# Feed-forward lists of a four-layer decoder: eight buffers of fetched rows with a lead of six, the best two experts by maxima, a BF16 inversion of places, and the weights in the last products

## What is computed

```python
# layer 0: h = rms-normed x
logits = h @ gate_w.T
top_w, top_i = top_k(softmax(logits), 2);  top_w /= top_w.sum(-1)
out[t] = sum over its two experts e of top_w * (silu(h @ w1[e].T) * (h @ w3[e].T)) @ w2[e].T
# layer 2
logits = x @ gate_w + gate_b
gw, top_i = softmax(top_k(logits, 2)), top_k(logits, 2)
out[t] = sum over its two experts e of gw * (gelu(x @ w1[e] + b1[e]) @ w2[e] + b2[e])
out[t] += gelu(x @ ws1 + bs1) @ ws2 + bs2
```

## Time and profile before

| | us |
|---|---|
| median of 3 runs | 3127.24 |
| the profiled execution | 3124.51 |
| its span | 3122.7 |
| PE busy | 2618.2 (84%) |
| DVE, ACT, POOL busy | 1691.0, 1106.2, 951.8 |
| layer 0: its feed-forward stage `Lists`, start to the end of the last product | 567 to 904 |
| layer 2: the same | 1946 to 2276 |

### The profile page before, as it was taken

The page is one execution under the profiler, slowest core; times in us unless marked ns, Lnnn a source line. Parts: engine busy times, 40 slices in busy tenths (PEclk is TensorE's granted clock), DMA queues, the critical chain, the costliest instruction groups (busy, mean ns, idle before and its releaser), DMA issues. The chain is left out here.

```text
span 3122.7 us, 39578 instructions
## 1 busy us (share of the span) xinstructions
PE 2618.2 (84%) x15186; PEld 1487.0 (48%) x15186; DVE 1691.0 (54%) x2983; ACT 1106.2 (35%) x2411; POOL 951.8 (30%) x953
## 2 busy tenths in 40 slices
PE   7999997656669998878888888866589999997999
PEld 3545555544444443446565655444443333333556
DVE  4454426411127871467777774412147878896623
ACT  1333333111115672233455553311134343433422
POOL 3332302032221100142544551122204444442265
PEclk8999989687878999989899998855669999999999
DMA  2000001100020002165222222100000000001033
GB/s 93 1 1 1 1 20 56 31 17 19 19 74 1 1 1 86 45 148 146 75 62 55 59 74 102 64 20 19 22 25 1 1 1 1 1 1 46 1 123 108
DMA packets 48353, 126.47 MB, mean 41 GB/s; under 512 B 11251, under 2 KB 26486, under 8 KB 44438
## 3 DMA queue, kind: packets, MB, share of 16 engines
q1 hardware_dynamic: 41638, 110.56, 11.2%
q0 software_dynamic: 6528, 13.38, 1.6%
HBM read 97.67 MB, written 26.23 MB: 40 GB/s over the span
## 5 line engine op out<-in xcount | busy, mean ns | idle before, releaser
L327 ACT ACTIVATE work<-ps 128x512 f32<-128x512 f32 (+5 forms) x959 | 496.2, 543 | 1130.3 <-PE ps L317 678.9
L317 PE MATMUL ps<-parts 64*128 64x512 f32 (+9 forms) x4368 | 829.7, 425 | 66.7 <-ACT fw_sb L328 15.0
L317 PEld LDWEIGHTS ps<-parts 32*128 32x128 f32 (+3 forms) x4368 | 450.5, 191 | 455.8 <-issue 227.3
L347 DVE TENSOR_REDUCE fw_sb<-ps 128x2 f32<-128x1024 f32 (+3 forms) x384 | 414.6, 1085 | 269.2 <-PE ps L317 268.7
L317 PE MATMUL ps<-fw_sb,work 128*32 128x128 f32 (+4 forms) x2174 | 397.7, 401 | 6.6 <-ACT work L327 2.2
L317 PE MATMUL ps<-work 128*32 128x256 f32 (+7 forms) x2524 | 380.2, 415 | 19.6 <-DVE work L331 11.1
L321 PE MATMUL ps<-wc_sb,work 128*128 128x128 f32 (+3 forms) x910 | 184.5, 328 | 236.8 <-DMA work<-scr_rows,work 189.6
L327 ACT ACTIVATE fw_sb<-ps 128x512 f32<-128x512 f32 (+5 forms) x394 | 204.6, 537 | 289.5 <-PE ps L317 246.9
L321 PEld LDWEIGHTS ps<-wc_sb,work 128*128 128x128 f32 (+3 forms) x910 | 129.0, 166 | 348.9 <-DMA work<-scr_rows,work 270.3
L344 DVE COPY work<-ps 128x512 f32<-128x512 f32 (+3 forms) x139 | 91.2, 660 | 342.8 <-PE ps L321 293.5
L317 PEld LDWEIGHTS ps<-fw_sb,work 128*32 128x32 f32 (+2 forms) x2174 | 219.2, 182 | 86.4 <-issue 72.4
(11 more groups left out here) (147 smaller groups left out, 3268.8 us busy)
## 6 DMA issues: line engine op xcount, KB each, us to landing
work<-scr_places SPq DMA_DIRECT2D x64, 256.0 KB
work<-scr_w SPq DMA_DIRECT2D x15, 1024.0 KB, 4.6
work<-scr_sk SPq DMA_DIRECT2D x64, 128.0 KB, 2.7
scr_sp<-wr_sb SPq DMA_DIRECT2D x64, 128.0 KB, 2.2
fw_sb<-in_f SPq DMA_DIRECT2D x1, 6528.0 KB, 19.3
fw_sb<-in_f SPq DMA_DIRECT2D x1, 5632.0 KB, 16.2
fw_sb<-in_f SPq DMA_DIRECT2D x1, 4608.0 KB, 18.3
scr_rows<-work SPq DMA_DIRECT2D x4, 1024.0 KB, 6.8
```

Of the source, the lines that this page charges most:

```text
L317: return self.e.matmul(o, l, r, start=start, stop=stop) if self.e else Unwritten()
L327: return self.e.activation(o, i, f, bias=bias, scale=scale)
L347: return self.e.tensor_reduce(o, i, AX.X, op, negate=neg) if self.e else Unwritten()
```

## The change

- `Lists` has eight buffers of fetched rows for four, six gathers ahead of the loop for three, and gathers n+6 for n+3; a buffer is free once `turn_pe` has read list n-8.
- The class `ListRoute` is gone. `choose_dve` finds the best expert by a maximum, takes it out, and finds the second the same way; where two are equal, the constant `order` picks the earlier one. ACT takes the exponential of 128x16 numbers in place of 128x128, behind all four copies of the tokens.
- `hot`, `of` and `V` are BF16, with the tokens innermost. `V` holds the token's number in two parts, which DVE adds afterwards, and no weights. Three BF16 constants are made once, by POOL in the first norm of the program.
- Weights: `weights_dve` runs behind the places. ACT makes 32 diagonal tiles from them, one in each turn of the loop from n = 2, and `back_pe` multiplies by these in place of the identity. `output_act` no longer scales.
- In layer 2 `prefix_pe` is set at 1, `inverted_pe` at 6 to 9 and `row_pe` at 11 to 14.

```diff
-        self.fetched = [k.event(f"fetched{l}_{i}", 16) for i in range(4)]
+        self.fetched = [k.event(f"fetched{l}_{i}", 16) for i in range(8)]
...
-        self.rows, self.X, self.S, self.out = ring(4, 128), ring(3, 128), ring(2, 512), ring(4, 128)
+        self.rows, self.X, self.S, self.out = ring(8, 128), ring(3, 128), ring(2, 512), ring(4, 128)
...
     def inverted_pe(self, e, q):
+        e.wait_ge(*k.made_v[t, "totals"])
         e.wait_ge(*k.made_v[t, "hot", q])
-        for i in range(8 * q, 8 * q + 8):
-            ins = e.matmul(r.Mb[1][:, 0:n], self.hot[:, tile(i)], self.V[:, n * i:n * i + n], start=i == 0, stop=i == 31)
+        for i in range(8):
+            n = 8 * q + i
+            ins = e.matmul(self.Mb[1][:, 0:2 * N], view(self.hot[:, 1024 * q + i:], [8, 128]), view(self.V[:, n:], [32, 2 * N]),
+                           start=n == 0, stop=n == 31)
...
     def shared_pe(self, e):
-            if i == 3:
+            if i == 1:
                 self.prefix_pe(e)
-            if 7 <= i < 11:
-                self.row_pe(e, i - 7)
-            if 10 <= i < 14:
-                self.inverted_pe(e, i - 10)
+            if 6 <= i < 10:
+                self.inverted_pe(e, i - 6)
+            if 11 <= i < 15:
+                self.row_pe(e, i - 11)
...
     def back_pe(self, e, c):
-                ins = e.matmul(k.ps[c][:, tile(i)], self.yt[:, at:at + 128], k.cst("id"), start=self.l == 0 and j == 0,
+                ins = e.matmul(k.ps[c][:, tile(i)], self.yt[:, at:at + 128], self.diag[:, tile(16 * j + 4 * c + i)], start=self.l == 0 and j == 0,
...
     def output_act(self, e, n):
-        e.activation(self.out[n % 4], self.Y, ACT.Copy, scale=self.w[:, n:n + 1]).then_inc(*k.made_a.up((t, "output", n)))
+        e.activation(self.out[n % 4], self.Y, ACT.Copy).then_inc(*k.made_a.up((t, "output", n)))
+
+    def diagonal_act(self, e, m):
+        e.wait_ge(*k.made_v[t, "weights"])
+        e.wait_ge(*k.summed[t, "inverted", 3])
+        e.activation(self.diag[:, tile(m)], k.cst("id"), ACT.Copy, scale=self.wk[:, m:m + 1]).then_inc(*k.made_a.up((t, "diagonal", m)))
...
+    def choose_dve(self, e):
+        e.wait_ge(*k.summed[t, "logits"])
+        self.step(e, e.reduce(self.m1, by_e(L), ALU.max))
+        self.step(e, e.tt(by_e(d), by_e(L), each(self.m1), ALU.subtract), (t, "logits"))
+        self.step(e, e.stt(by_e(tie), by_e(d), 0.0, order, ALU.is_equal, ALU.mult))
+        self.step(e, e.reduce(self.c16, by_e(tie), ALU.max))
+        self.step(e, e.tt(by_e(one), by_e(tie), each(self.c16), ALU.is_equal))
+        self.step(e, e.stt(d, one, -BIG, d, ALU.mult, ALU.add))
+        self.step(e, e.reduce(self.m2, by_e(d), ALU.max))
+        self.step(e, e.tt(by_e(d2), by_e(d), each(self.m2), ALU.subtract), (t, "second"))
+        self.step(e, e.stt(by_e(tie), by_e(d2), 0.0, order, ALU.is_equal, ALU.mult))
+        self.step(e, e.reduce(self.c16, by_e(tie), ALU.max))
+        self.step(e, e.tt(by_e(two), by_e(tie), each(self.c16), ALU.is_equal))
+        self.step(e, e.tt(self.mask, one, two, ALU.add), (t, "mask"))
...
     def places_dve(self, e):
+        self.step(e, e.tt(of, each(self.j), view(k.firstb[:, :], [32, N], [1, 32]), ALU.is_equal))
+        e.tt(V(0), of, each(k.pairb[:, 0:32]), ALU.mult).then_inc(*k.made_v.up((t, "lower numbers")))
+        e.tt(V(1), of, each(k.pairb[:, 32:64]), ALU.mult).then_inc(*k.made_v.up((t, "upper numbers")))
...
     def pool(self, e):
-        for n in range(3):
+        for n in range(6):
             self.fetch_pool(e, n)
         e.wait_ge(*k.made_v[t, "to"])
         for n in range(N):
-            if n + 3 < N:
-                self.fetch_pool(e, n + 3)
+            if n + 6 < N:
+                self.fetch_pool(e, n + 6)
             self.send_pool(e, n)
...
@@ class FirstNorm(PickNorm): pool
+        for o, name, n, m in ((k.seqb, "seq", 128, 8), (k.firstb, "firsts", 39, 32), (k.pairb, "pairs", 64, 1)):
+            e.copy(view(o[:, :], [m, n], [1, m]), view(k.cst(name), [1, n], [0, m])).then_inc(*k.made_g.up((self.tag, o.name)))
```

More of the change, by code:

```diff
@@ L3364, in __getitem__, with __init__ @@
         return self.of[name][name]
[L3367 to L3386, removed]
 class Lists(Stage):
     N = 39
-    def __init__(self, k, l, A, route, x, big):
+    def __init__(self, k, l, A, x, big):
         super().__init__(f"lists{l}")
-        self.k, self.l, self.r, self.x = k, l, route, x
+        self.k, self.l, self.x, self.Mb, self.steps = k, l, x, [k.ps[6], k.ps[7]], 0
         self.width = 448 if l == 0 else 512
@@ L3448, in logits_pe @@
     def logits_pe(self, e):
[L3449 to L3452, removed]
+        k, bank, plain = self.k, self.Mb[1], self.l == 0
+        if not plain:
+            e.matmul(bank[:, 0:128], k.cst("ones")[0:1, :], view(k.wt(2, "gateb"), [0, 16], [1, 8]), stop=False)
         for i in range(16):
[L3454 to L3456 removed]
+            ins = e.matmul(bank[:, 8 * i:8 * i + 8], self.x[:, tile(i)], k.wt(self.l, "gate"), start=plain, stop=plain or i == 15)
+        ins.then_inc(*k.summed.up((self.tag, "logits")))
     def tokens_pe(self, e, c):
@@ L3566, in back_pe @@
         e.wait_ge(*self.came[c])
+        e.wait_ge(*k.made_a[t, "diagonal", 31])
         for i in range(4):
@@ L3669, in act @@
                 self.output_act(e, n - 2)
+            if 2 <= n < 34:
+                self.diagonal_act(e, n - 2)
     def step(self, e, ins, key=None):
-        self.r.step(e, ins, key)
+        k = self.k
+        self.steps += 1
+        key = key or (self.tag, "chain", self.steps)
+        ins.then_inc(*k.made_v.up(key))
+        e.wait_ge(*k.made_v[key])
+    def choose_dve(self, e):
+        k, t, L = self.k, self.tag, self.Mb[1]
+        by_e, each = lambda a: view(a, [8, 16], [1, 8]), lambda a: view(a, [1, 16], [0, 8])
+        order = view(k.cst("order"), [0, 16], [1, 8])
+        d, d2, tie, one, two = self.d, self.d2, self.tie, self.sel[:, 0:128], self.sel[:, 128:256]
+        e.wait_ge(*k.summed[t, "logits"])
[11 more added lines that the diff above has]
+        self.step(e, e.tt(self.mask, one, two, ALU.add), (t, "mask"))
@@ L3774, in fetch_pool @@
         k, t = self.k, self.tag
-        e.wait_ge(*k.summed[t, "turned", n - 4])
-        e.gather(self.rows[n % 4], self.table, self.at[:, n:n + 1]).then_inc(*self.fetched[n % 4].up(n))
+        e.wait_ge(*k.summed[t, "turned", n - 8])
+        e.gather(self.rows[n % 8], self.table, self.at[:, n:n + 1]).then_inc(*self.fetched[n % 8].up(n))
     def send_pool(self, e, n):
```

144 lines of the change are left out of this document (70 added, 74 removed).

## The result

| | before | after |
|---|---|---|
| median | 3127.56 us (4 runs, 3119.09 to 3132.26) | 2791.03 us (4 runs, 2779.13 to 2802.17) |
| profiled execution, its span | 3124.51, 3122.7 | 2788.2, 2786.4 |
| granted clock over the span | 0.886 | 0.931 |
| layer 0, loop | 273.6 | 122 |
| layer 2, loop | 261.0 | 105 |

The ratio is 0.8926 with a 95% interval of 0.8884 to 0.8969. The forecast was 2796 us.

What follows compares the result with a forecast made beforehand. The prediction took a ring of output, scatter, gather and PE's turn, with PE's lowered clock, to bound both loops. Terms −19.5 − 149.6 − 158 − 6.2 + 2.6 = −330.7 us gave 2796 us, range 2778 to 2890.

Steps and rivals of the forecast that it cites:

- The loops: Loops over 39 lists: six lists of lead bring layer 0 from 273.6 to 124 us, layer 2 from 261.0 to 103.
- Layer 2's turn: Layer 2's loop: PE's turn 2.3 us at full clock, GpSimd slower, so the loop ends at 101.5 us or later.
- Layer 0 before the loop: Layer 0's start: new mask search, DVE wide operations of 9.1 us and cheaper BF16 inversion save 19.5 us.
- Layer 2 before the loop: Layer 2's inversion in PE's stream: four quarters of 1.91 us become 0.35 us each, 6.2 us less.
- The first norm: End of the first norm's stage: three more POOL casts behind the 2048 cast cost 2.6 us, at worst 5.
- Diagonals: Products behind the loops: diagonals replace the identity in 64 instructions of the same shape, costing 0.
- The stages behind: Stages behind the loops: their end should not move in length.
- (a): Rival, layer 2's loop: PE stays at half clock, 4.6 us a turn, loop 181 us, total 2874 us; chance 0.11.
- (b): Rival, both layers' loops: PE stays at half clock, layer 0's loop 233 us, total 2983 us; chance 0.04.
- (c): Rival, both loops: scatter and gather transfers serialise, 4.9 us a turn, 191 us each, total 2951 us; chance 0.05.
- (d): Rival, both loops: more indirect transfers in flight each take longer, kernel gets slower, 3307 us; chance 0.02.
- (e): Rival, both loops: the lead does nothing, only the starts and the cast count, 3104 us; chance 0.02.

Runs made afterwards that it cites:

- lead_only: Kernel before with only eight buffers of fetched rows and a gather lead of six; 2820.4 us, ratio 0.904.
- lead3: Kernel after with four buffers and a gather lead of three, all other edits kept; 3091.9 us, ratio 0.9911.
- pool1: Kernel after with one memset of 128x512 and a wait for it behind each scatter on GpSimd; 2815.6 us, ratio 0.9017.
- hot_rows: Kernel after with the BF16 one-hot array of places laid out by token tile, its columns side by side; 2797.1 us, ratio 0.8958.
- v_rows: Kernel after with the 78 columns of V for one token tile side by side; 2783.0 us in one run.
- no_diagonal: Kernel after without the 32 diagonals on ACT, identity used again, weights left out of the result; 2802.1 us, ratio 0.8974.
- after_again: Kernel after run once more, unchanged, beside the kernel with three small edits; 2820.2 us, ratio 0.9009.
- pool2: Kernel after with two memsets of 128x512, each waited for, behind each scatter on GpSimd; 2858.2 us, ratio 0.9154.
- lead4: Kernel after with five buffers and a gather lead of four; 2822.3 us, ratio 0.9045.

## Why the prediction was right, and where not

- **The loops** (−149.6 and −158) are the change, and both terms stand: −151.2 and −156.1 us by the traces. lead_only and lead3 show from both sides that the lead is the cause. The turn in layer 0, 3.0 us with 2.93 as the bound, is 2.94.
- **Layer 2's turn** was mis-sized, and the 103 us came out near 104.9 by luck. The prediction had 2.3 us for PE's turn, and it is 2.46. The step at fault is the 1.44 us from a transposition to the next product up: in the loop it is 1.60 (1860.49 to 1862.09), and 0.86 from there to the next transposition, which is the 1.02 less the overlap, as forecast. The 1.44 was read in the earlier trace rows from the turn just before the first scatter; the kernel after also has it in that one turn and 1.60 from the next on. What adds the 0.16 us is not shown. The forecast then took GpSimd's 101.5 us for the bound, over 96 us for PE alone. But PE's own stream fills the 104.9 us: 8.0 us for the first three turns, some 2.47 for each of 36, and 7.9 behind them, where the prediction had 5. GpSimd would have been done some 4 us earlier, as its waits at the loop's end and pool1 show.
- **Layer 0 before the loop** (−19.5) came to −20.45 us, 41.24 to 20.79 from the logits to the first transposition, but by errors that cancel in part. DVE's wide operations took 4.8 us and not 9.1, so the rule on 16-bit data that the prediction cited from the Trainium skill (VectorE: DVE Perf Modes, The perf-mode tier table) holds in this trace, and hot_rows shows a limit of it: the same operations at 1.16 us once an operand repeats one number along its innermost run. PE's products took 0.141 us and not 0.043, 4.5 us in all, and ended last, so that the places stood 3.4 us behind DVE's last quarter and not 1.1. The step at fault is the price from the mask's products, which are other work in columns, weights and layout; v_rows shows that the layout of V's columns is 0.06 us of the 0.10 between them. And the first rows came 3.8 us after the first gather's start, where the kernel before has 2.8 (612.57 to 615.36) and v_rows 2.9, so that about 1 us of the gain was lost again.
- **Layer 2 before the loop** (−6.2) was off by the same price: four quarters save 2.7 us, not 6.2, and the stretch from the first product of the stage to the first transposition fell from 53.0 to 49.6 us, −3.4.
- **The first norm** (+2.6): the casts run for 2.4 us behind the 2048 cast, and moving them away gave 2.3 us. Right.
- **Diagonals, 0**: right, by no_diagonal; the 64 products took 0.7 us more in layer 0, with the identity as well.
- **The stages behind "should not move in length"**: they did. From the last scatter of layer 0 to the start of layer 2's stage, 1058.2 us became 1050.4, with the same instructions. The drift belongs to the execution and not to the change: from the start of layer 0's last scatter to the first quarter of the inversion in layer 2 the same code took 1072.6 us in the first trace of after,

```profile
720.49 0.97 POOL L372 DMA_INDIRECT scr_back<-work  x1 [0.75 <-ACT work L328]
...
1793.12 1.24 PE L318 MATMUL ps<-work 128*128 128x78 bf16 x8
```

and 1090.3 us in that of pool1 (722.81 to 1813.09). In after_again, run to measure this, the stretch to the start of layer 2's stage took 1054.5 us; the traces with the same code there lie between 1050.4 and 1068.1 us, and the kernel before, with 1058.2, lies among them. The feed-forward part of layer 1 alone took 113.1 us at a clock of 0.97 before and 118.7 us at 0.90 after. The sum of the prediction, −330.7 us, and the 336.3 us that the span lost are therefore closer than two executions can tell.
- **The rivals.** (a) and (b), half the clock, did not come; even pool2, which leaves PE idle for a quarter of layer 2's loop, has 0.97 of the clock there. The Trainium skill's rule that speaks for (a) (TensorE: Matmul & The Clock Gate, A second HAM failure mode) is not borne out here: the idles of PE in pool1 and pool2, up to 1.8 us in a turn, left the clock at 0.97 and 0.98. In this program it fell where PE has pauses of some 3 us, as in the earlier trace rows. (c) and (d), transfers that hinder each other, fall with the landings of 2.6 and 2.3 us. (e) falls with the loops.

## What to carry to other kernels

Where an in-order queue holds both the writes that depend on a result and the reads that feed it, count the turns from the result to the reads that stand behind it: the ring's latency divided by that number is the least time of a turn. Give more turns than the median latency asks for, because late single transfers cost time as soon as there is no slack (lead4 in layer 0); a lead of six left no wait, and five was not tried. A low granted clock beside such pauses is mostly a symptom: filling the pauses gave 57 us, opening the ring 307. And look at both operands' innermost steps before BF16 is priced, on DVE and on PE, since either can lose what the type gives.

## What was not expected of the hardware

- Eight BF16 products of 128x128 by 78 columns take 1.24 us with the columns of the moving operand 64 bytes apart, 1.31 us with 16 bytes, and 0.63 us with them side by side; with the moving columns 64 bytes apart, the step of the weights (16 bytes or none) changes nothing (1.24 and 1.23 us).
- A BF16 tensor_tensor on DVE takes 0.62 us for 1024 numbers with stepless runs of eight, and 1.16 us where one operand stands still along the innermost run.
- PE kept 0.97 of its clock with an idle of about 1 us in most turns of 3.7 us (pool2, layer 2), and had 0.6 to 0.8 of it over loops with 3 us of idle in turns of some 7 (before, lead3).
- The delays of ACT and DVE in layer 2, every 9.1 us on one chip, above, whose cause stays open.
